# Order of the vector engine's operations in the stage that builds dense arrays of a graph network, and where loop bounds are loaded

## The chip, the cores and the metric

The kernel runs on one core of a Trainium2 chip. The metric is the device time of one execution in microseconds, lower is better. Five engines work side by side, each through its own program in order: PE (TensorE, matrix products into the PSUM banks), DVE (VectorE), ACT (ScalarE), POOL (GpSimd) and SP (SyncE, which issues DMAs). They meet at semaphores only.

## The reference

Four graph layers follow each other on a graph of 6250 nodes and 200,000 edges with 64 features a node. Each is added to its input and normalized over the features. Cut to what matters here:

```python
def prop(x):                                  # layer 0, Chebyshev, three times
    return segment_sum((x * norm)[src], dst, 6250) * norm
h = relu(concat(x[src], x[dst], edge_attr, u) @ W1 + b1)   # layer 1
agg = segment_sum(h, dst, 6250)
msg = edge_weight[:, None] * h[cols]          # layer 2, twice
h = segment_sum(msg, rows, num_segments=n)    # then a batch norm in Lorentz space
agg = segment_sum(h[src] * norm[:, None], dst, 6250)       # layer 3, graph convolution
```

The edges come sorted by dst, and dst is drawn as 6250 times a square of a uniform number, so nodes with a low number have many edges and the others few. The kernel turns the edge list into two dense arrays first: how often each source occurs for each destination (counts, for layers 0 and 3), and the sum of the edge weights for each pair (for layer 2). The sums over edges are then matrix products with these arrays.

## The kernel before, in words

The change lies in the stage that builds the two arrays (`build_dense` on DVE and PE, a loop on ACT, one on POOL). A **group** is five destinations; a source is split into a high part (50 values) and a low part (125), and a group has one PSUM bank. Two groups (`QUAD`) are a **block**, two blocks a **unit**: 1250 groups, 625 blocks, 313 units. The eight banks hold two units.

Edges stand 128 to a column. For the first column of every group everything is loaded ahead in `firsts`. A group with many edges needs more columns: these are the extra slots, **mores**, numbered `s` over the whole stage, each of which serves both groups of a block. How many a block has stands in the table `offs_sb`, which each engine reads into registers (`offs_of`, line 399, through `loads`, a TENSOR_LOAD whose line is 392). POOL picks the columns of a more out of the lists (`take`, line 655) into a ring of eight slots; it loads sixteen values of its own table for every five blocks (line 392 too).

The work of one unit, in the order of the engines' programs:

- DVE, `unit`: waits until `first_used` tells that PE is through with the unit two before, which used the same of two buffers (`first_planes`). Then `one_hots` (line 930, one operation of 1500 elements a partition) compares the keys with 0 to 124. Then `products` (line 937) multiplies the one-hots of the low part by three parts of the weight: one operation of 750 elements for each of the two blocks. Then the mores in order, each with `one_hots` (750 elements), a wait for it, and `products` (750). The one-hots of more `s` wait for `more_used`, that is until PE is through with more `s - 2`, and for POOL.
- PE, `unit`: loads the offsets once in two units, ahead of the first. `counts_of` (line 1653, one matmul of 250 columns a group, four a unit) needs the one-hots, and that ACT has copied the bank's last content out (`block_copied`). `weights_of` (line 1661, six matmuls a group, 24 a unit) needs the products; the last matmul of a block raises `first_used`. A more has two matmuls of line 1653 and twelve of line 1661, and the last raises `more_used`.
- ACT, `batch`: for each of five blocks waits until PE is through with it and its mores, and copies the weights (line 1424) and the counts (line 1425) out of the banks. It loads five offsets at the begin of a batch, and copies the degrees (line 1428) at its end. SP stores each batch of weights to DRAM, and counts after 25 blocks.

DVE loads its offsets once in two units too, ahead of the first one's one-hots. Semaphores raised ahead by POOL set the depths: `first_used` by 4 (two units), `more_used` by 2, `more_products` by 8, `block_copied` by 4.

## Time and profile before

| | |
|---|---|
| Median of 3 runs | 6696.05 us (6693.28 to 6703.47) |
| Profiled execution | 6737.52 us, span 6735.8 us |
| Mean granted TensorE clock | 0.761 |
| Busy over the span | PE 65%, PEld 50%, DVE 41%, POOL 30%, ACT 15% |
| The stage of the change | 190 us to 1995 us of the span |

How to read it. PE is the matmuls, PEld the weight loads beside them. The page cuts the span into 40 slices of 168 us; the stage of the change is slices 2 to 12. Busy counts an engine's operations, not its register work, branches, loads of registers (TENSOR_LOAD) or waits. In a timeline a row is one or several operations merged: start, time from the first's start to the last's end, engine, line, what is written and read, number, and in brackets the idle time before it with what ended it ("issue" is time in which the engine waited for nothing that the profile shows, such as its own register loads). T and X are the tiles in which the buffers lie: T those of units, X those of mores.

### The profile page before, as it was taken

What the parts mean: (1) busy time and instruction counts of PE and PEld (TensorE: products, weight loads), DVE (VectorE), ACT (ScalarE), POOL (GpSimd) and SP (SyncE); (2) the same over time, 40 slices, a digit from 0 to 9 for tenths busy, and PEclk for the clock granted to TensorE, in tenths of its full rate; (3) what the DMA queues carried; (4) which work ended last, traced back from release to release, by engine and by line L of the source; (5) the groups of instructions that cost most, each with busy time, mean ns of one, the idle gap of its engine ahead of it and who ended that gap; (6) DMA issues with size and microseconds to landing.
All of it is one profiled execution on the core that took longest, in us unless ns stands there. A gap on an engine that the chain in (4) does not pass through costs nothing.

```text
span 6735.8 us, 125070 instructions
## 1 busy us (share of the span) xinstructions
PE 4407.9 (65%) x39288; PEld 3374.0 (50%) x39289; DVE 2743.6 (41%) x4741; ACT 1043.5 (15%) x2060; POOL 2010.8 (30%) x2919
## 2 busy tenths in 40 slices
PE   1788888777669999625555555555555567657475
PEld 0566666666559899523333333333333343323275
DVE  8877777665551111323333333333333320020323
ACT  1012223355550000100000000000000000000100
POOL 2433332211000000055656656565656510000000
PEclk6899999988888999755555555555555569989887
DMA  2012333456766898352222222222222259969575
GB/s 74 9 56 71 105 105 112 127 176 218 221 215 267 345 377 348 121 98 61 61 60 61 61 61 61 61 61 61 61 60 61 61 199 418 371 284 418 230 291 194
DMA packets 443170, 1061.56 MB, mean 158 GB/s; under 512 B 127013, under 2 KB 285543, under 8 KB 414216
## 3 DMA queue, kind: packets, MB, share of 16 engines
q1 hardware_dynamic: 390985, 1003.20, 41.7%
q0 software_dynamic: 52096, 57.38, 4.2%
q8 instruction: 30, 0.49, 0.0%
q14 instruction: 59, 0.48, 0.0%
HBM read 815.58 MB, written 244.81 MB: 157 GB/s over the span
## 4 chain that ended last, share of the span: by engine, by line
PE 23%; issue 19%; DVE 19%; another core or an unknown queue 16%; DMA 9%; DVEq 6%; ACT 4%; ACTq 2%; SPq 1%; POOLq 1%; POOL 0%
PE banks L1627 12%; DMA T<-dense_w 8%; DVE X L930 4%; PE banks L1661 3%; DVE T L930 3%; PE banks L1712 2%; DVEq L392 2%; DVE WORK L1048 1%; ACTq L392 1%; DVE WORK L1032 1%; DVE WORK L1046 1%; PE banks L1653 1%; DVEq L930 1%; PE banks L1599 1%
## 5 line engine op out<-in xcount | busy, mean ns | idle before, releaser
L695 POOL DMA_INDIRECT WORK<-table,idx x1568 | 1523.2, 971 | 1880.2 <-DVE idx L1054 875.5
L1627 PE MATMUL banks<-WORK,T 125*128 125x192 bf16 (+1 forms) x10000 | 834.4, 247 | 61.8 <-DVE WORK L1098 61.8
L1627 PEld LDWEIGHTS banks<-WORK,T 125*128 125x128 bf16 (+1 forms) x10000 | 832.0, 99 | 64.2 <-issue 47.5
L1588 PE MATMUL banks<-W1c,WORK 128*128 128x128 f32 x1568 | 474.3, 429 | 463.3 <-issue 461.8
L1712 PE MATMUL banks<-T,WORK 125*64 125x391 f32 (+1 forms) x3200 | 575.3, 500 | 228.1 <-DMA T<-dense_w 186.2
L1584 PE MATMUL banks<-T,WORK 128*128 x1568 | 275.5, 293 | 639.3 <-issue 319.8
L1588 PEld LDWEIGHTS banks<-W1c,WORK 128*128 128x128 f32 x1568 | 382.5, 320 | 504.0 <-issue 503.8
L655 POOL TENSOR_TENSOR T<-T 128x6 f32 x1182 | 365.3, 331 | 837.1 <-DVE X L937 694.3
L1661 PE MATMUL banks<-X 128*128 128x125 bf16 x7092 | 549.2, 226 | 62.9 <-DVE X L937 57.6
L1661 PE MATMUL banks<-T 128*128 128x125 bf16 (+1 forms) x7500 | 576.6, 239 | 0.2 <-DVE T L937 0.2
L1661 PEld LDWEIGHTS banks<-T 128*128 128x128 bf16 x7500 | 538.6, 120 | 51.1 <-DVE T L937 42.4
L1661 PEld LDWEIGHTS banks<-X 128*128 128x128 bf16 x7092 | 460.2, 116 | 201.8 <-DVE X L937 192.2
L1584 PEld LDWEIGHTS banks<-T,WORK 128*128 128x128 bf16 x1568 | 219.3, 140 | 669.9 <-issue 664.2
L1424 ACT ACTIVATE WORK<-banks 125x504 f32<-125x504 f32 x625 | 378.1, 605 | 1106.0 <-PE banks L1661 981.4
L1712 PEld LDWEIGHTS banks<-T,WORK 125*64 125x64 f32 x3200 | 253.0, 137 | 549.4 <-issue 432.2
L1597 PE MATMUL banks<-WORK 128*128 128x128 bf16 x1568 | 429.3, 274 | 118.3 <-DVE WORK L1048 113.2
L1482 ACT ACTIVATE WORK<-WORK 128x512 bf16<-128x512 f32 x196 | 123.5, 630 | 2386.2 <-issue 1301.2
L1599 PE MATMUL banks<-WORK 128*64 128x128 bf16 x1568 | 464.6, 296 | 5.3 <-issue 5.3
L1032 DVE TENSOR_TENSOR WORK<-banks,WORK 128x512 f32<-128x512 f32 x196 | 135.6, 692 | 745.8 <-remote 624.1
L930 DVE TENSOR_TENSOR T<-X,NORM 128x1500 bf16<-128x1500 bf16 x313 | 294.5, 941 | 331.6 <-issue 183.4
L1653 PE MATMUL banks<-T 128*128 128x250 bf16 x1250 | 221.5, 298 | 313.7 <-DVE T L930 193.6
L1017 DVE TENSOR_TENSOR ACC<-ACC,banks 128x128 f32 x196 | 55.9, 285 | 808.6 <-remote 776.4
(369 smaller groups left out, 4777.7 us busy)
## 6 DMA issues: line engine op xcount, KB each, us to landing
T<-dense_c SPq DMA_DIRECT2D x200, 1562.5 KB, 8.4
T<-dense_w SPq DMA_DIRECT2D x200, 782.0 KB, 10.3
T<-dense_w SPq DMA_DIRECT2D x200, 780.5 KB, 10.4
dense_w<-WORK SPq DMA_DIRECT2D x125, 1093.8 KB
WORK<-rel_rows SPq DMA_DIRECT2D x197, 256.0 KB
WORK<-in_eaT SPq DMA_DIRECT2D x392, 128.0 KB
dense_c<-T SPq DMA_DIRECT2D x13, 3125.0 KB, 14.8
dense_c<-ACC SPq DMA_DIRECT2D x12, 3125.0 KB, 15.1
```

The costliest lines, as they stand in the source:

```text
L655: last = nc.gpsimd.tensor_tensor(quads[:, ds(slot, 1), :, t].rearrange("p s k -> p (s k)"), lists[:, :, ds(at[t], 1)].rearrange("p k c -> ...
L695: nc.gpsimd.indirect_dma_start(out=g_sb[:, u, c * D:(c + 1) * D], out_offset=None, in_=table, in_offset=bass.IndirectOffsetOnAxis(ap=idx[: ...
L930: return V.tensor_tensor(plane[:, 0:pairs * HOTS].rearrange("p (k n t) -> p k n t", n=LO, t=QUAD), iota2[:, 0:LO, :].unsqueeze(1).to_broad ...
L1424: C.activation(dense_out[0:LO, b0, 2 * b:2 * b + 2, :], both[:, :, KEYS:KEYS + 2 * WCOLS], ACT.Copy)
L1584: T.matmul(z, lhsT, QW12[:, ds(at * 2, P)], start=c in (0, 2), stop=False, skip_group_check=True)
L1588: last = T.matmul(z_sums[:, v, 2 * c * P:2 * (c + 1) * P].rearrange("p (c h f) -> p h c f", c=2, f=D)[:, 0, :, :], ea_sb[:, v, c * P:(c + ...
L1597: T.matmul(banks[:, v, 0:P], parts[:, v, c, 0:2 * D], hots[:, v, c // 2, :, c % 2], start=c == 0, stop=False, skip_group_check=True)
L1599: last = T.matmul(banks[0:D, v, 0:P], parts[:, v, c, 2 * D:3 * D], hots[:, v, c // 2, :, c % 2], start=False, stop=c == CHUNKS - 1, skip_g ...
L1627: last = T.matmul(banks[0:cols, 2 * u + s, 0:3 * D], a_rows[:, u, h * WAYS + s * LO:h * WAYS + s * LO + cols], x123[:, h, :], start=h == 0 ...
L1653: T.matmul(banks[:, bank, 0:KEYS], lows_view(plane, h)[:, t, :], hots_view(plane, h)[:, t, :], start=begins, stop=False, skip_group_check= ...
L1661: last = T.matmul(banks[:, bank, to - low:to + LO + high], keys_view(plane, h)[:, t, j, :], plane[:, first - QUAD * low:past + QUAD * high ...
L1712: last = [T.matmul(banks[c * D:(c + 1) * D, 4 * h + j, 0:n], lt[:, y, :], aw_sb[0:LO, 4 * y + 2 * h + c, j * PIECE:j * PIECE + n], start=f ...
```

## The change

On DVE the program is turned round. `products` takes all blocks of a unit in one operation of 1500 elements. The one-hots of unit 0 come ahead of the loop; in the loop come the one-hots of unit u+1, the products of unit u, in every second unit the load of offsets, and the mores of unit u. Of a pair of mores come both one-hots, then both products; a single more is done as before. `first_products` is raised once a unit, and PE waits for it once a unit. PE loads its offsets between the weights of the first of two units and their mores. ACT loads ten offsets for two batches at once in place of five for each.

```diff
--- before.py
+++ after.py
@@ -931,42 +931,59 @@
                                            iota2[:, 0:LO, :].unsqueeze(1).to_broadcast([P, 3 * pairs, LO, QUAD]),
                                            keys.unsqueeze(2).to_broadcast([P, 3 * pairs, LO, QUAD]), ALU.is_equal)
 
-                def products(plane, pairs, h, weights):
-                    first = products_of(pairs) + h * WEIGHTS
-                    low = plane[:, h * HOTS + QUAD * 2 * LO:(h + 1) * HOTS].rearrange("p (n t) -> p n t", t=QUAD)
-                    return V.tensor_tensor(plane[:, first:first + WEIGHTS].rearrange("p (k n t) -> p k n t", k=3, t=QUAD)[:, :, 0:LO, :],
-                                           low.unsqueeze(1).to_broadcast([P, 3, LO, QUAD]),
-                                           weights.unsqueeze(2).to_broadcast([P, 3, LO, QUAD]), ALU.mult)
-
-                def more(s, x):
-                    quad = quads[:, ds(s & (QRING - 1), 1), :, :].rearrange("p s k t -> p (s k) t")
+                def products(plane, pairs, weights):
+                    low = plane[:, 0:pairs * HOTS].rearrange("p (h k n t) -> p h k n t", k=3, n=LO, t=QUAD)[:, :, 2, :, :]
+                    return V.tensor_tensor(plane[:, products_of(pairs):planes_of(pairs)].rearrange("p (h k n t) -> p h k n t", k=3, n=WCOLS, t=QUAD)[:, :, :, 0:LO, :],
+                                           low.unsqueeze(2).to_broadcast([P, pairs, 3, LO, QUAD]),
+                                           weights.rearrange("p (h k) t -> p h k t", k=3).unsqueeze(3).to_broadcast([P, pairs, 3, LO, QUAD]), ALU.mult)
+
+                def quad_of(s):
+                    return quads[:, ds(s & (QRING - 1), 1), :, :].rearrange("p s k t -> p (s k) t")
+
+                def more_one_hots(s, x):
                     dve.wait_ge(quad_taken, s + 2)
                     dve.wait_ge(more_used, s + 1)
-                    one_hots(more_planes[:, x, :], 1, quad[:, 0:3, :]).then_inc(more_hots, 1)
+                    one_hots(more_planes[:, x, :], 1, quad_of(s)[:, 0:3, :]).then_inc(more_hots, 1)
+
+                def more_weights(s, x):
                     dve.wait_ge(more_hots, s + 1)
-                    products(more_planes[:, x, :], 1, 0, quad[:, 3:6, :]).then_inc(more_products, 1)
-
-                def unit(u, v, offs):
-                    plane, pairs = first_planes[:, v, :], UNIT // QUAD
+                    products(more_planes[:, x, :], 1, quad_of(s)[:, 3:6, :]).then_inc(more_products, 1)
+
+                pairs = UNIT // QUAD
+
+                def first_one_hots(u, v):
                     dve.wait_ge(first_used, u * pairs + pairs)
-                    one_hots(plane, pairs, firsts[:, 0, ds(u * pairs, pairs), :, :].rearrange("p b k t -> p (b k) t")).then_inc(first_hots, 1)
+                    one_hots(first_planes[:, v, :], pairs, firsts[:, 0, ds(u * pairs, pairs), :, :].rearrange("p b k t -> p (b k) t")).then_inc(first_hots, 1)
+
+                def first_weights(u, v):
                     dve.wait_ge(first_hots, u + 1)
-                    for h in range(pairs):
-                        products(plane, pairs, h, firsts[:, 1, ds(u * pairs + h, 1), :, :].rearrange("p b k t -> p (b k) t")).then_inc(first_products, 1)
+                    products(first_planes[:, v, :], pairs, firsts[:, 1, ds(u * pairs, pairs), :, :].rearrange("p b k t -> p (b k) t")).then_inc(first_products, 1)
+
+                def mores(offs):
                     dve.wait_ge(more_used, offs[0] + SLOTS)
                     dve.sem_inc(mores_begun, 1)
                     for h, (begin, past) in enumerate(zip(offs, offs[1:])):
                         with dve.If(past > begin):
                             with dve.Fori(begin, past, 2) as s:
-                                more(s, 2 * h)
                                 with dve.If(past > s + 1):
-                                    more(s + 1, 2 * h + 1)
-
+                                    for j in range(2):
+                                        more_one_hots(s + j, 2 * h + j)
+                                    for j in range(2):
+                                        more_weights(s + j, 2 * h + j)
+                                with dve.Else():
+                                    more_one_hots(s, 2 * h)
+                                    more_weights(s, 2 * h)
+
+                first_one_hots(dve.snap(0, min_val=0, max_val=0), 0)
                 with dve.Fori(0, UNITS // 2) as i:
-                    offs = offs_of(dve, i * 4, 5)
                     for v in range(2):
-                        unit(i * 2 + v, v, offs[2 * v:2 * v + 3])
-                unit(UNITS - 1, 0, offs_of(dve, BLOCKS - 1, 2))
+                        first_one_hots(i * 2 + (v + 1), 1 - v)
+                        first_weights(i * 2 + v, v)
+                        if v == 0:
+                            offs = offs_of(dve, i * 4, 5)
+                        mores(offs[2 * v:2 * v + 3])
+                first_weights(dve.snap(UNITS - 1, min_val=0, max_val=UNITS - 1), 0)
+                mores(offs_of(dve, BLOCKS - 1, 2))
                 end()
 
             def begin_rounds():
@@ -1409,9 +1426,8 @@
                 C.activation(to[:, 1, 0, :], got[:, 2, :], ACT.Copy).then_inc(firsts_copied, 1)
             end()
 
-            def batch(n, j, turn):
+            def batch(n, j, turn, past):
                 nth, slot, b0 = j // BATCHES // 2, j // BATCHES % 2, j % 2
-                past = offs_of(act, n * BATCH + 1, BATCH)
                 for b in range(BATCH):
                     d = (j % BATCHES * BATCH + b) * QUAD * GROUP
                     if b == 0:
@@ -1428,10 +1444,12 @@
                 C.activation(degp[0:LO, ds(n * SPAN, SPAN), :], dense_out[0:LO, b0, :, 0:2 * WCOLS:2 * WCOLS - 1], ACT.Copy).then_inc(degs_moved, 1)
 
             with act.Fori(0, STREAMS // 4) as i:
-                for j in range(4 * BATCHES):
-                    batch(i * (4 * BATCHES) + j, j, i)
+                for j in range(0, 4 * BATCHES, 2):
+                    past = offs_of(act, (i * (4 * BATCHES) + j) * BATCH + 1, 2 * BATCH)
+                    for k in range(2):
+                        batch(i * (4 * BATCHES) + (j + k), j + k, i, past[k * BATCH:])
             for j in range(BATCHES):
-                batch((STREAMS - 1) * BATCHES + j, j, STREAMS // 4)
+                batch((STREAMS - 1) * BATCHES + j, j, STREAMS // 4, offs_of(act, ((STREAMS - 1) * BATCHES + j) * BATCH + 1, BATCH))
             act.wait_ge(degs_moved, STREAMS * BATCHES)
             end()
             R = load(act, rounds_i[0:1, 0:1], 1, P)
@@ -1673,19 +1691,21 @@
                         last = weights_of(plane, 1, 0, t, bank + t)
                     last.then_inc(more_used, 1)
 
-                def unit(u, v, offs):
-                    plane, blocks = first_planes[:, v, :], len(offs) - 1
+                def unit(u, v, blocks):
+                    plane = first_planes[:, v, :]
                     pe.wait_ge(first_hots, u + 1)
                     for h in range(blocks):
                         pe.wait_ge(block_copied, u * 2 + (h + 1))
                         for t in range(QUAD):
                             counts_of(plane, h, t, UNIT * v + QUAD * h + t, True)
+                    pe.wait_ge(first_products, u + 1)
                     for h in range(blocks):
-                        pe.wait_ge(first_products, u * 2 + (h + 1))
                         for t in range(QUAD):
                             last = weights_of(plane, UNIT // QUAD, h, t, UNIT * v + QUAD * h + t)
                         last.then_inc(first_used, 1)
-                    with pe.If(offs[blocks] > offs[0]):
+
+                def mores(v, offs):
+                    with pe.If(offs[-1] > offs[0]):
                         for h, (begin, past) in enumerate(zip(offs, offs[1:])):
                             with pe.If(past > begin):
                                 with pe.Fori(begin, past, 2) as s:
@@ -1694,10 +1714,13 @@
                                         more(s + 1, 2 * h + 1, UNIT * v + QUAD * h)
 
                 with pe.Fori(0, UNITS // 2) as i:
-                    offs = offs_of(pe, i * 4, 5)
                     for v in range(2):
-                        unit(i * 2 + v, v, offs[2 * v:2 * v + 3])
-                unit(UNITS - 1, 0, offs_of(pe, BLOCKS - 1, 2))
+                        unit(i * 2 + v, v, 2)
+                        if v == 0:
+                            offs = offs_of(pe, i * 4, 5)
+                        mores(v, offs[2 * v:2 * v + 3])
+                unit(UNITS - 1, 0, 1)
+                mores(0, offs_of(pe, BLOCKS - 1, 2))
                 end()
 
             def dense_pass(l):
```

## Rows read from the trace of the kernel before

**Rows 1.** The page's part 1: busy us (share of the span) and instructions.

```profile
PE 4407.9 (65%) x39288; PEld 3374.0 (50%) x39289; DVE 2743.6 (41%) x4741; ACT 1043.5 (15%) x2060; POOL 2010.8 (30%) x2919
```

**Rows 2.** Windows: length; PE, PEld, DVE, ACT, POOL busy (count); PEclk; DMA; GB/s.

```profile
190.00:550.00 360.00, 305.90 (x3696) 235.02 (x3697) 279.13 (x518) 44.99 (x88) 143.05 (x468) 0.97 0.11 34
550.00:900.00 350.00, 304.39 (x3714) 240.00 (x3711) 271.39 (x486) 97.88 (x192) 118.75 (x370) 0.98 0.30 93
900.00:1455.00 555.00, 446.43 (x5306) 365.96 (x5306) 389.68 (x662) 210.04 (x421) 142.59 (x417) 0.93 0.41 131
1455.00:1995.00 540.00, 374.06 (x4315) 325.57 (x4312) 303.32 (x465) 321.06 (x676) 27.01 (x52) 0.88 0.68 213
```

**Rows 3.** The same windows, DVE line 930 alone: length, busy (count), PEclk, DMA.

```profile
190.00:550.00 360.00, 142.26 (x244) 0.97 0.11 34
550.00:900.00 350.00, 138.45 (x221) 0.98 0.30 93
900.00:1455.00 555.00, 193.36 (x283) 0.93 0.41 131
1455.00:1995.00 540.00, 145.79 (x156) 0.88 0.68 213
```

**Rows 4.** Timeline, two pairs of mores of the first unit.

```profile
224.76 0.93 PE L1661 MATMUL banks<-X 128*128 128x125 bf16 x12 [0.23 <-DVE X L937]
...
225.92 0.92 PE L1661 MATMUL banks<-X 128*128 128x125 bf16 x12
225.99 0.55 DVE L930 TENSOR_TENSOR X<-X,T 128x750 bf16<-128x750 bf16 x1
...
226.68 0.38 PE L1653 MATMUL banks<-X 128*128 128x250 bf16 x2
226.69 0.55 DVE L937 TENSOR_TENSOR X<-X,T 128x750 bf16<-128x750 bf16 x1
227.16 0.54 DVE L930 TENSOR_TENSOR X<-X,T 128x750 bf16<-128x750 bf16 x1
...
227.30 0.93 PE L1661 MATMUL banks<-X 128*128 128x125 bf16 x12 [0.24 <-DVE X L937]
...
228.53 0.55 DVE L930 TENSOR_TENSOR X<-X,T 128x750 bf16<-128x750 bf16 x1
```

**Rows 5.** Groups by line, last stretch: busy, mean ns | idle before, releasers.

```profile
L930 DVE TENSOR_TENSOR T<-X,NORM 128x1500 bf16<-128x1500 bf16 x153 | 144.1, 942 | 212.2 <-PE banks L1661 134.4 <-issue 77.3
...
L1653 PE MATMUL banks<-T 128*128 128x250 bf16 x610 | 115.4, 306 | 163.3 <-DVE T L930 75.8 <-ACT ACC L1425 40.4 <-ACT T L1425 35.5
...
L1653 PEld LDWEIGHTS banks<-T 128*128 128x128 bf16 x610 | 51.6, 108 | 197.1 <-ACT T L1425 78.1 <-ACT ACC L1425 63.1 <-issue 47.9
```

**Rows 6.** Line 392, register loads, last stretch: ns min/median/max, first and last start.

```profile
L392 DVEq TENSOR_LOAD <-X x76: 583/1974/3059, 1459.7 to 1988.5; - x76
L392 ACTq TENSOR_LOAD <-X x61: 540/2275/5810, 1457.0 to 1984.9; - x61
...
L392 POOLq TENSOR_LOAD <-X x52: 1057/2718/5303, 1454.9 to 1684.5; - x52
```

**Rows 7.** Timeline of ACT, its first copy after a load.

```profile
1755.43 0.59 ACT L1424 ACTIVATE WORK<-banks 125x504 f32<-125x504 f32 x1 [5.49 <-issue]
```

**Rows 8.** Timeline of units without mores.

```profile
1759.06 0.53 PE L1661 MATMUL banks<-T 128*128 128x126 bf16 x4
...
1759.73 0.94 DVE L930 TENSOR_TENSOR T<-X,NORM 128x1500 bf16<-128x1500 bf16 x1 [4.09 <-PE banks L1661]
...
1760.81 1.01 DVE L937 TENSOR_TENSOR T<-T,NORM 128x750 bf16<-128x750 bf16 x2
...
1761.96 0.63 PE L1653 MATMUL banks<-T 128*128 128x250 bf16 x4 [0.46 <-issue]
...
1762.43 1.63 PE L1661 MATMUL banks<-T 128*128 128x125 bf16 x24
```

**Rows 9.** Timeline of PE, weights of a unit at the lower clock.

```profile
1785.65 2.72 PE L1661 MATMUL banks<-T 128*128 128x125 bf16 x24
```

## The prediction, made before the change was built

> **What bounds the kernel now.** I read the page first: no engine is busy for more than 65% of the span [rows 1], so the answer lies in a stage. The change touches only the stage that builds the dense arrays, from 190 us to 1995 us, so I cut this stage into four stretches [rows 2]. Line 930 runs once for each unit and once for each extra slot, which I call a more [rows 3]. PE runs 28 matmuls for a unit and 14 for a more, so its count over 14 is twice the units plus the mores: 3696/14 = 264 in the first stretch, less 244, is 20 units and 224 mores. The others hold 44, 96 and 153 units with 177, 187 and 3 mores. A unit takes 18, 8.0, 5.8 and 3.5 us in the four.
>
> With mores, two engines hand to each other [rows 4]. PE ends a more's weights at 225.69 (224.76 + 0.93), DVE starts one-hots at 225.99, products 0.70 later, PE starts their weights 0.61 after that (227.30) and ends 0.93 later. That is 0.30 + 0.70 + 0.61 + 0.93 = 2.54 us, and the one-hots two mores apart start 2.54 apart (225.99, 228.53). So the wait on the more two back closes this loop; it is no engine's busy time.
>
> Without mores (the last stretch), three share the bound [rows 5]. DVE's idle before a unit's one-hots is 134.4 us for PE and 77.3 us "issue", which holds the load of five offsets (median 1.97 us there [rows 6]). PE's weight loads wait 78.1 + 63.1 = 141 us for ACT, and its matmuls 75.8 us for DVE. ACT stands for up to 5.49 us at a time where it loads [rows 7].
>
> **The change part by part.** (1) **The next unit's one-hots ahead of this unit's products.** DVE runs in program order. The one-hots of unit u+1 wait until PE is through the weights of unit u-1 (they share a buffer). Before, nothing but unit u+1 itself stood behind that wait; now the products of unit u stand behind it, and PE's weights of unit u wait for them. So a loop closes over one unit. The weights of u-1 end; 0.14 us later the one-hots of u+1 start (1759.06 + 0.53 to 1759.73 [rows 8]) and take 0.94. The products don't depend on them and start 0.08 before their end, as the one-hots at 227.16 do behind products of 0.55 that began at 226.69 [rows 4]; so 0.86. The products as one operation of 1500 elements get 0.94, that of the one-hots with as many elements; bounds 1.01 (the two now, overlapped) and 1.10 (twice 0.55). PE's weights of the first block used to follow the first 0.55 and now wait for all of it. Then 0.06 (0.61 less 0.55) and the weights 1.63 [rows 8]. Sum: 0.14 + 0.86 + 0.94 + 0.06 + 1.63 = **3.63 us a unit** as a floor, where 540/153 = 3.53 is the mean now, stalls included. PE's counts, 0.63, lie in the gap of 2.00 beside it.
>
> On top of the floor: the clock. At the lower clock the weights take 2.72 [rows 9]; the granted clock of the stretch is 0.88 [rows 2], so 24% of it is at 1.2 GHz, 0.24 x 1.09 = 0.26; I take 0.2, since some of it falls in idle time. PE's load and ACT, below, get 0.1 and 0.2. So 4.13 us a unit, 153 x 4.13 = 632 us against 540: **+92 us**. Lower bound 3.63 throughout, +15; upper bound with ACT's whole wait kept, 141/153 = 0.92 instead of 0.2, 4.85 us, +202.
>
> (2) **Mores in pairs: one-hots, one-hots, products, products.** The second one-hots of a pair need the more just before the pair to be used, and the first products now stand behind them. The loop over a pair becomes: release 0.30, one-hots to products 0.47 (independent), products to weights 0.61, weights to the next counts 0.76 (225.92 to 226.68), two counts 0.24 (half of the 0.47 that four take, 1761.96 to 1762.43 [rows 8]), weights 0.92: **3.30 us for two mores** instead of 2.54 [rows 4]. In exchange DVE's own time for a pair falls by 0.46 (four starts 0.47 apart instead of 0.70 and 0.47 in turn), which helps only where PE is not waited for. POOL, which waits for products to reuse a slot, gets the first of a pair 0.47 later; it may be eight slots ahead, so I add nothing (without that cover 0.24 a more). A unit of two pairs, from the end of its own weights: DVE had time for the first pair while PE did the weights, so PE does it at its rate, 0.24 + 0.92 + 0.76 + 0.24 = 2.16; the second ends 3.30 later, 5.46; the next unit's counts start 0.16 before that and its weights end 0.47 + 1.63 later, 7.40. PE now loads its offsets between weights and mores, where the mores wait for it. Where it loads today it stands for 0.46 [rows 8]; more branches follow here, so I double that, an estimate: 0.9 in two units, 0.45 a unit, 7.9 in all. First stretch: 20 x 7.9 + (224 - 80)/2 x 3.30 = 158 + 238 = 396 against 360, **+36 us**. Second: 44 x 7.9 + 0.5 x 3.30 = 350, **0**. By the same steps a unit with three mores takes 6.6, one with two 4.6, one with one or none about 4.0. The third stretch runs from three down to none, 1.9 on average, mixed: 5.2 against 5.8, 96 x 5.2 = 499 against 555, **-56**. Bounds of these three together: +36 if few mores gain nothing, -75 if the first stretch loses nothing and the gain is a third larger.
>
> (3) **DVE's load behind products.** DVE loads once in two units, 0.58 to 3.06 us [rows 6], and idles. Behind the queued one-hots and products (0.86 + 0.94) it is hidden but for the longest. The trace has no DVE load beside a running operation, so the cover could be missing; then it costs what it costs now. In the last stretch this gives nothing in any case: DVE waits there for PE in the loop of (1), with 1.8 us a unit to spare. The gain of the third stretch contains it.
>
> (4) **ACT loads ten offsets once in ten blocks, not five in five.** Sixteen values cost POOL 1.06 us and five cost 0.54 to 0.58 [rows 6], so undisturbed two loads become one for 0.3 us less in five units. But ACT's median is 2.28 and its longest 5.81 while the stores run; if ten values cost twice five, nothing is saved and the stall comes in one piece. The counts of a unit may start 1.4 us late in the loop of (1) (2.00 less 0.63) before it shows. I take 0.2 a unit, between 0 and 0.92. The Trainium skill ("Runtime: NRT & Kernel Launch", Instruction fetch mechanics) gives about 200 ns a register for such loads; five more values would be 1.0 us more, where the rows give 0.04 us a value ((1.06 - 0.58)/11). By that rule ACT's stall comes in one piece, which is rival C; the rows of undisturbed loads speak against it, ACT's own median of four times its shortest for it.
>
> Sum: 92 + 36 + 0 - 56 = **+72 us**. The profiled execution took 6737.52 (span 6735.8), so it would be 6810; the median of the runs is 6696.05, 0.6% below, and the same difference gives **6768 us**.
>
> **The rivals.** A, the forecast, 57%: own range +30 to +130. B, **faster**: PE is so far ahead that the wait on unit u-1 doesn't bite, and DVE's hidden load and ACT's fewer loads show. A unit would be bound by PE's 0.63 + 1.63 or ACT's 2.10 of work (321/153 [rows 2]) with its loads, about 3.0: 153 x 3.0 = 459, -81, with -56 and +36 together -101: 6595. For it: DVE's idle of 77.3 us on issue. Against: it decides only if PE's weights of u-1 end more than 1.8 us before PE could start those of u, and the order on DVE leaves no way to that. A weaker form, the floor with no stall (+15) and the mores at their lower bound (-75), gives 6636. Together 13%. C, **ACT takes over**: loads of ten cost twice, 5 to 11 us, more than two units of banks can cover; the last stretch goes to 4.85 us a unit, +202 in place of 92: 6878. 15%. D, **the lower clock**: PE idles 1.4 us in each unit; if the clock stayed at 1.2 GHz, weights of 2.72 make a unit 3.63 + 1.09 = 4.72, +182 in place of 92: 6858. 5%. E: gains and costs cancel within 0.2%, 10%.
>
> **How the numbers follow.** A measurement can tell about 0.2%, 13 us, from no change. Faster 0.13 (B), same 0.10 (E), slower 0.77 (A, C, D). The range leaves out most of B and the top of C: 6680 to 6880.
>
> **What would show it.** In the last stretch DVE's one-hots should follow PE's last weights by 0.14 with products right behind, PE's weights should start 0.06 behind products, and starts of one-hots should stand 3.6 to 4.2 apart; DVE's idle on "issue" should be gone and PE's idle on DVE grow from 75.8 to over 150 us. In the first unit, pairs should repeat every 3.30 us. ACT should load 65 times in the stage instead of 125; loads over 5 us each point to C. It is wrong if the last stretch is under 3.5 us a unit, or pairs stay at 2.5.

## The result and the profile after

The changed kernel takes **6889.8 us** (median of 4 runs, 6887.6 to 6892.4); before measured beside it 6696.7. The ratio is 1.0287, 95% interval 1.0269 to 1.0305: slower by 193 us, where +72 was forecast, and 10 us above the end of the range. The profiled execution spans 6886.9 us. The page's part 1 of after, to hold against [rows 1]:

```profile
PE 4362.3 (63%) x39288; PEld 3375.5 (49%) x39289; DVE 2658.6 (39%) x4428; ACT 1047.1 (15%) x2060; POOL 2042.4 (30%) x2919
```

PE and ACT have the work of before, DVE has 313 operations and 85 us less; what has grown is waiting. Windows of after, the same four stretches moved to where their units now run (columns as in [rows 2]):

```profile
190.00:585.00 395.00, 289.44 (x3608) 236.32 (x3609) 259.42 (x488) 42.50 (x83) 129.24 (x459) 0.98 0.10 31
585.00:945.00 360.00, 289.41 (x3731) 246.33 (x3730) 255.32 (x446) 96.78 (x192) 128.85 (x377) 0.98 0.28 87
945.00:1505.00 560.00, 436.94 (x5324) 363.06 (x5321) 368.63 (x571) 209.71 (x422) 169.67 (x422) 0.95 0.42 131
1505.00:2175.00 670.00, 405.20 (x4302) 335.98 (x4302) 275.60 (x310) 322.62 (x666) 24.08 (x51) 0.81 0.54 170
```

The matmuls of the four (16,965, in [rows 2] 17,031) count out to nearly the same work; the first stretch ends a few us before its twentieth unit does. In the rows of after, lines 936, 1671, 1679, 1440 and 1441 are what lines 937, 1653, 1661, 1424 and 1425 are in before. The last stretch has grown by 130 us and its granted clock has fallen from 0.88 to 0.81.

For an exact comparison I take as marks the start of the first products of units 0, 20, 64, 160 and 312 in each trace; "slot" below is the time from one mark to the next. Before: **353, 354, 554, 535**, sum 1796. After: **397, 360, 562, 668**, sum 1987, so +44, +6, +8, +133: 191 of the 193 us lie in the stage. Differences of a few us between two kernels in one slot say nothing by themselves: each is one profiled execution.

**The loop over one unit is there as forecast.** Timeline of after, last stretch, at a place where ACT isn't loading (ACT, POOL and PEld rows left out):

```profile
1887.01 0.62 PE L1671 MATMUL banks<-T 128*128 128x250 bf16 x4
...
1887.31 0.94 DVE L930 TENSOR_TENSOR T<-X,NORM 128x1500 bf16<-128x1500 bf16 x1 [1.86 <-PE banks L1679]
...
1888.17 0.93 DVE L936 TENSOR_TENSOR T<-T,NORM 128x1500 bf16<-128x1500 bf16 x1
...
1889.16 1.65 PE L1679 MATMUL banks<-T 128*128 128x125 bf16 x24 [1.54 <-DVE T L936]
...
1890.97 0.94 DVE L930 TENSOR_TENSOR T<-X,NORM 128x1500 bf16<-128x1500 bf16 x1 [1.86 <-PE banks L1679]
```

From one-hots to products 0.86, to PE's weights 0.99, these 1.65, and 0.16 later the next one-hots: 3.66 us a unit. The forecast's floor was 3.63. In 67 of the 152 units of the last slot the one-hots follow each other at 3.66 to within 0.02, and in none at less than 3.64. Before, they followed at 2.27 in the commonest case, the second unit of two, for which DVE has nothing to load.

**ACT's stall and the clock lie on top of it.** A load of ten offsets runs here between two rows of ACT:

```profile
1759.49 2.22 PE L1679 MATMUL banks<-T 128*128 128x125 bf16 x24 [0.68 <-DVE T L936]
1761.51 1.03 PE L1671 MATMUL banks<-T 128*128 128x250 bf16 x4
...
1763.70 2.71 PE L1679 MATMUL banks<-T 128*128 128x125 bf16 x24 [1.16 <-DVE T L936]
...
1769.04 0.59 ACT L1440 ACTIVATE WORK<-banks 125x504 f32<-125x504 f32 x1 [10.27 <-issue]
...
1770.16 0.60 PE L1671 MATMUL banks<-T 128*128 128x250 bf16 x2 [3.75 <-ACT ACC L1441]
...
1771.52 2.61 PE L1679 MATMUL banks<-T 128*128 128x125 bf16 x24
...
1774.28 0.94 DVE L930 TENSOR_TENSOR T<-X,NORM 128x1500 bf16<-128x1500 bf16 x1 [5.92 <-PE banks L1679]
```

ACT stands for 10.27 us, longer than the two units whose banks are free last, and PE idles 3.75 us for it. And PE, with gaps in front of its counts and of its weights, does a unit's weights in 2.71 us (1.2 GHz) in place of 1.65 (2.4 GHz). The loads of after in this stretch, columns as in [rows 6]:

```profile
L392 DVEq TENSOR_LOAD <-X x76: 580/1358/2966, 1512.4 to 2174.9; - x76
...
L392 ACTq TENSOR_LOAD <-X x32: 559/5381/10277, 1514.0 to 2166.3; - x32
```

32 loads in place of 61 (in the whole stage 65 in place of 125, as said), but the median has gone from 2.28 to 5.38 us.

**Idle time of the last stretch.** Waits of DVE, 1510 to 2160 us (us in total, times, longest):

```profile
DVE T L930 <- PE banks L1679: 384.1, 147, 9.7
```

Groups of PE's matmuls and of DVE's one-hots, 1505 to 2175 us, columns as in [rows 5]:

```profile
L1679 PE MATMUL banks<-T 128*128 128x125 bf16 x2416 | 289.5, 250 | 126.1 <-DVE T L936 125.6
...
L930 DVE TENSOR_TENSOR T<-X,NORM 128x1500 bf16<-128x1500 bf16 x152 | 143.5, 944 | 393.1 <-PE banks L1679 393.1
...
L1671 PE MATMUL banks<-T 128*128 128x250 bf16 x608 | 121.7, 324 | 137.3 <-ACT T L1441 56.2 <-ACT ACC L1441 52.7 <-DVE T L930 21.7
```

DVE's 77.3 us on "issue" of [rows 5] are gone, but nothing is won by that: DVE waits 393 us for PE here (134.4 before), while PE waits 125.6 + 21.7 = 147 us for DVE (before 75.8), just short of the 150 that I named. Each waits for the other in turn: that is the closed loop.

**The pairs** of the first unit, timeline (POOL and PEld left out), against [rows 4]:

```profile
225.91 0.89 PE L1679 MATMUL banks<-X 128*128 128x125 bf16 x12
...
227.11 0.55 DVE L930 TENSOR_TENSOR X<-X,T 128x750 bf16<-128x750 bf16 x1 [0.41 <-POOL T L655]
227.58 1.00 DVE L936 TENSOR_TENSOR X<-X,T 128x750 bf16<-128x750 bf16 x2
...
228.18 0.92 PE L1679 MATMUL banks<-X 128*128 128x125 bf16 x12 [1.02 <-DVE X L936]
...
229.16 0.89 PE L1679 MATMUL banks<-X 128*128 128x125 bf16 x12
...
230.36 0.55 DVE L930 TENSOR_TENSOR X<-X,T 128x750 bf16<-128x750 bf16 x1 [0.41 <-POOL T L655]
```

Release 226.80 to 227.11, products 0.47 later, weights 0.60 later, and so on: 230.36 - 227.11 = 3.25 us a pair, forecast 3.30. The row names POOL as what ended the wait, but the wait for `more_used` passes 0.04 us behind the end of PE's weights both times, so it was PE.

### The profile page after: what moved, and what is told of

Its sections match the earlier page's. It is cut to its first block, busy times and chain, and to the rows that moved or that the text cites. A ratio compares the mean times of both kernels' runs of the same rounds, so it can differ in the third digit from the quotient of the medians.

```text
span 6886.9 us, 124604 instructions
## 1 busy us (share of the span) xinstructions
PE 4362.3 (63%) x39288; PEld 3375.5 (49%) x39289; DVE 2658.6 (39%) x4428; ACT 1047.1 (15%) x2060; POOL 2042.4 (30%) x2919
## 4 chain that ended last, share of the span: by engine, by line
PE 28%; DVE 19%; another core or an unknown queue 18%; issue 12%; DMA 9%; DVEq 5%; ACTq 3%; ACT 2%; POOLq 2%; SPq 1%; POOL 1%
PE banks L1645 12%; DMA T<-dense_w 8%; PE banks L1679 7%; ACTq L392 2%; PE banks L1735 2%; DVEq L392 2%; DVE WORK L1065 2%; DVE T L936 2%; DVE X L936 2%; DVE WORK L1049 1%; PE banks L1617 1%; DVE X L930 1%; PE banks L1615 1%; DVE WORK L1052 1%
## 5 line engine op out<-in xcount | busy, mean ns | idle before, releaser
L655 POOL TENSOR_TENSOR T<-T 128x6 f32 x1182 | 395.8, 357 | 862.8 <-DVE X L936 606.1
L1679 PEld LDWEIGHTS banks<-X 128*128 128x128 bf16 x7092 | 487.8, 116 | 255.6 <-DVE X L936 247.4
L1615 PEld LDWEIGHTS banks<-WORK 128*128 128x128 bf16 x1568 | 163.5, 104 | 911.3 <-issue 768.4
L1606 PE MATMUL banks<-W1c,WORK 128*128 128x128 f32 x1568 | 434.0, 432 | 141.7 <-issue 140.6
L930 DVE TENSOR_TENSOR X<-X,T 128x750 bf16<-128x750 bf16 x591 | 319.3, 552 | 359.5 <-PE banks L1679 169.1
L1606 PEld LDWEIGHTS banks<-W1c,WORK 128*128 128x128 f32 x1568 | 366.4, 325 | 134.4 <-issue 133.8
```

Source lines behind the costliest of these rows:

```text
L655: last = nc.gpsimd.tensor_tensor(quads[:, ds(slot, 1), :, t].rearrange("p s k -> p (s k)"), lists[:, :, ds(at[t], 1)].rearrange("p k c -> ...
L930: return V.tensor_tensor(plane[:, 0:pairs * HOTS].rearrange("p (k n t) -> p k n t", n=LO, t=QUAD), iota2[:, 0:LO, :].unsqueeze(1).to_broad ...
L1606: last = T.matmul(z_sums[:, v, 2 * c * P:2 * (c + 1) * P].rearrange("p (c h f) -> p h c f", c=2, f=D)[:, 0, :, :], ea_sb[:, v, c * P:(c + ...
L1615: T.matmul(banks[:, v, 0:P], parts[:, v, c, 0:2 * D], hots[:, v, c // 2, :, c % 2], start=c == 0, stop=False, skip_group_check=True)
L1679: last = T.matmul(banks[:, bank, to - low:to + LO + high], keys_view(plane, h)[:, t, j, :], plane[:, first - QUAD * low:past + QUAD * high ...
```

## The experiments

Each ratio is to the kernel before on the same chip. The slots are 0 to 20, 20 to 64, 64 to 160, 160 to 312, in us. Code that only follows from an edit (definitions split, line moves) is left out of the diffs. Extra values that ACT loads are not used. The first four kernels ran on a chip on which the kernel before takes 6157.9 us in all, the others on chips on which it takes 6731 to 6740. The stage takes the same on all: where a kernel leaves a slot's work alone, the slot comes out within 6 us of before's (ACT ten alone 353, 354, 558; pairs alone 536 in the last). Outside the slots up to 13 us more separate a kernel from before (branches alone, 104 by the ratio and 91 in the slots); no run explains these.

| kernel | ratio (95%) | slots | sum against 1796 |
|---|---|---|---|
| order alone | 1.0056 (1.0040 to 1.0073) | 348, 339, 536, 600 | +27 |
| pairs alone | 1.0157 (1.0140 to 1.0174) | 410, 367, 572, 536 | +89 |
| one operation alone | 1.0033 (1.0022 to 1.0045) | 362, 358, 560, 534 | +18 |
| ACT ten alone | 1.0126 (1.0109 to 1.0143) | 353, 354, 558, 600 | +69 |
| branches alone | 1.0156 (1.0138 to 1.0173) | 389, 381, 580, 537 | +91 |
| DVE's load alone | 0.9972 (0.9960 to 0.9984) | 352, 352, 555, 522 | -15 |
| after, ACT five | 1.0197 (1.0180 to 1.0214) | 399, 356, 553, 612 | +124 |
| after, PE's load first | 1.0281 (1.0264 to 1.0298) | 399, 348, 557, 679 | +187 |
| after, mores as before | 1.0178 (1.0160 to 1.0195) | 346, 344, 543, 668 | +105 |
| order and DVE's load | 1.0011 (1.0000 to 1.0021) | 344, 334, 527, 596 | +5 |
| ACT from a multiple of four | 0.9982 (0.9973 to 0.9992) | 354, 352, 552, 518 | -20 |
| ACT eight | 0.9954 (0.9939 to 0.9969) | 354, 354, 552, 505 | -31 |
| ACT eight, DVE's load | 0.9948 (0.9934 to 0.9961) | 350, 352, 554, 505 | -35 |
| the same, PE's load | 0.9935 (0.9920 to 0.9950) | 351, 353, 550, 502 | -40 |
| split order | **0.9880** (0.9863 to 0.9896) | 346, 334, 523, 501 | -92 |

### One part of the change at a time, on the kernel before

**The order alone.**

```diff
+first_one_hots(0, 0)
 with dve.Fori(0, UNITS // 2) as i:
     offs = offs_of(dve, i * 4, 5)
     for v in range(2):
+        first_one_hots(i * 2 + (v + 1), 1 - v)
         unit(i * 2 + v, v, offs[2 * v:2 * v + 3])
```

`unit` here has products and mores only.

> The kernel before with one edit: the one-hots of unit u+1 come ahead of the products of unit u. Products stay two operations, mores, DVE's, PE's and ACT's loads stay as before. I count the stage in units 0 to 19, 20 to 63, 64 to 159 and 160 to 311; before they take 353, 354, 554 and 535 us, in the changed kernel 397, 360, 562 and 668. Theory (the loop over one unit): the last stretch gets a floor of 0.14 + 0.86 + 0.55 + 0.06 + 1.63 = 3.24 us a unit (PE's weights start behind the first of the two products) and with clock and ACT about 3.8, so 580 us, +45; the first three move by less than 10 each; in all +30 to +60, about 6740. Rival (ACT's loads of ten cause the loss, the order is harmless or hides something): the last stretch stays within 10 of 535 or falls.

Measured: -5, -15, -18, +65. Units with mores gain from the order, units of the last slot lose 0.43 us each. The floor is there: 49 of 151 distances between one-hots in the last slot lie at 3.25 to 3.32, forecast 3.24. What lies on top of it was put too low, 3.8 a unit where 3.95 was measured; the granted clock of the slot is 0.82, before 0.88.

**Pairs alone.** The `mores` of the diff above, with `Else`, on the old order.

```diff
-more(s, 2 * h)
 with dve.If(past > s + 1):
-    more(s + 1, 2 * h + 1)
+    for j in range(2):
+        more_one_hots(s + j, 2 * h + j)
+    for j in range(2):
+        more_weights(s + j, 2 * h + j)
+with dve.Else():
+    more_one_hots(s, 2 * h)
+    more_weights(s, 2 * h)
```

> The kernel before with one edit: of a pair of mores both one-hots come first, then both products; a single more has its own branch. Theory (the two mores' loop closes one more earlier): pairs of the first unit repeat every 3.3 us instead of 2.54, +40 us in the first stretch, +10 in the second. For the third stretch, where the forecast failed, two theories: if the extra branch and register work of the single more costs DVE's time (0.5 us a single), it takes +20 to +40; if the trouble there is the order over units or PE's load, it stays within 10. Last stretch 535 unchanged.

Measured: +57, +13, +18, +1, a pair every 3.25 us in most cases.

**The products of a unit in one operation.**

```diff
-for h in range(pairs):
-    products(plane, pairs, h, ...).then_inc(first_products, 1)
+products(plane, pairs, ...).then_inc(first_products, 1)
```

> The kernel before with one edit: the products of a unit in one operation of 1500 elements, one semaphore step a unit, PE waits for it once. Theory: an operation of 0.94 us in place of two that take 1.01 together, so DVE gains 0.07 a unit, and PE's first weights start 0.39 later; where DVE or ACT sets the pace neither shows: within 15 us of before in all. Rival (the merged operation alone costs 0.39 a unit wherever PE waits for DVE): +20 to +60, most of it in the last two stretches.

Measured: +9, +4, +6, -1, ratio 1.0033: a small loss of 18 us, just above the 15 expected, in the slots with mores. PE begins a unit's weights later, and DVE saves 0.07 us.

**ACT loads ten.**

```diff
-for j in range(4 * BATCHES):
-    batch(i * (4 * BATCHES) + j, j, i)
+for j in range(0, 4 * BATCHES, 2):
+    past = offs_of(act, (i * (4 * BATCHES) + j) * BATCH + 1, 2 * BATCH)
+    for k in range(2):
+        batch(i * (4 * BATCHES) + (j + k), j + k, i, past[k * BATCH:])
```

> The kernel before with one edit: ACT loads ten offsets for two batches instead of five for each. In the changed kernel these loads took 2.6, 5.4 and 10.1 us (shortest, median, longest in the last stretch), against 0.54, 2.28 and 5.81. Theory (a load costs by the value and its stall comes in one piece): the last stretch grows by 20 to 60 us, the first two not at all, ACT's loads as in the changed kernel. Rival (half as many loads help, since ACT has fewer stops): the last stretch falls by 10 to 40.

Measured: 0, 0, +4, **+65**. Its loads and its clock (0.82, before 0.88):

```profile
L392 ACTq TENSOR_LOAD <-X x33: 560/5369/10012, 1460.2 to 2053.7; - x33
```

```profile
1455.00:2055.00 600.00, 388.64 (x4299) 337.93 (x4297) 300.88 (x462) 321.43 (x668) 25.94 (x52) 0.82 0.61 191
```

So this part costs much the same without the new order. The four parts add up to +61, +2, +10, +130 against the whole change's +44, +6, +8, +133, which also moves DVE's and PE's loads. In the first slot they don't add: 17 us are missing.

**The branches alone.** Mores in the old order, but with the branches of the pairs.

```diff
-more(s, 2 * h)
 with dve.If(past > s + 1):
+    more(s, 2 * h)
     more(s + 1, 2 * h + 1)
+with dve.Else():
+    more(s, 2 * h)
```

> The kernel before with the branch form of the changed one, the order of operations kept: if a pair is left, one-hots, products, one-hots, products, else the single more. The pairs edit alone gave 410, 367, 572 and 536 us against 353, 354, 554 and 535. Theory A (order makes the pairs slow, branches make the singles slow): first stretch within 5 of 353 with pairs at 2.54, third stretch +10 to +20. Theory B (all comes from the order): all within 5.

Measured: **+36, +27, +26, +2**, as much as the pairs together, with the same operations in the same order. Its timeline (PE, PEld, POOL left out):

```profile
226.59 0.54 DVE L930 TENSOR_TENSOR X<-X,T 128x750 bf16<-128x750 bf16 x1
...
227.29 0.55 DVE L937 TENSOR_TENSOR X<-X,T 128x750 bf16<-128x750 bf16 x1
...
228.28 0.55 DVE L930 TENSOR_TENSOR X<-X,T 128x750 bf16<-128x750 bf16 x1 [0.44 <-POOL T L655]
...
228.98 0.55 DVE L937 TENSOR_TENSOR X<-X,T 128x750 bf16<-128x750 bf16 x1
```

Products to the next pair's one-hots take 0.99 us, before 0.68: the jump over the `Else`, the loop's jump and the test now lie between them, where before the test stood beside a running operation. A pair takes 2.85 in place of 2.54. Put on top of this, pairing itself gives +21, -14, -8. The gain is not where I forecast it, in units with few mores: in the third slot a unit with three takes 7.47 here and 7.23 with pairs alone, one with two 6.05 and 6.09, one with one 4.84 and 4.89. Of the 28 units with two mores, 27 have one for each block, so they hold no pair at all. Beside the gain the branches cost more than all of it.

### Parts undone in the changed kernel

**After, with ACT's loads of five.** The inverse of the fourth diff.

> The changed kernel with ACT's loads as before, five offsets for each batch. The four stretches (units 0 to 19, 20 to 63, 64 to 159, 160 to 311) take 397, 360, 562 and 668 us in the changed kernel. Theory (the parts add up: ACT's ten alone gave +65 in the last stretch, the order alone +65): the last stretch falls by 55 to 70, to about 605, the others by less than 5. Rival (behind the loop over one unit ACT has room, so its loads cost nothing there; the forecast's 0.2 us a unit): it falls by less than 30.

Measured: last slot 668 to 612, clock of the stretch 0.81 to 0.87. Ten against five offsets is 56 us here, 65 on before.

**After, with PE's load ahead of the unit's counts.**

```diff
 with pe.Fori(0, UNITS // 2) as i:
+    offs = offs_of(pe, i * 4, 5)
     for v in range(2):
         unit(i * 2 + v, v, 2)
-        if v == 0:
-            offs = offs_of(pe, i * 4, 5)
         mores(v, offs[2 * v:2 * v + 3])
```

> The changed kernel with PE's load of offsets back at the begin of two units, ahead of their counts, instead of between weights and mores. Theory (in the third stretch the mores wait for that load on PE, and DVE's entry to the next mores waits for PE to be through with them): the third stretch falls from 562 by 15 to 40, the second from 360 by 10 to 20, the last by less than 10. Rival (the third stretch's loss is DVE's branches and the pairs): under 10 in each.

Measured, against after: +2, -12, -5, +11. Where it stands makes no difference in the sum; the ratio's interval overlaps that of after. The sum hides two effects in the third slot: with the load first, a unit with one more takes 4.76 in place of 5.13, and one with none 4.38 in place of 3.98.

**After, with the mores as before**: one after the other, old branches.

> The changed kernel with one part undone: the mores are done one after the other with the branches of before, everything else as changed. Theory (the pair and its branches cost the first two stretches, and their sum with order, loads and one operation is additive): stretches of the changed kernel 397, 360, 562, 668 go to 345-360, 338-355, 525-545 and 660-670, ratio to before 1.016 to 1.022, nearly all of what is left in the last stretch. Rival (in the third stretch the wait of DVE for all earlier mores, with PE's load ahead of them, is what took the expected gain): third stretch stays at 550 or more.

Measured: 346, 344, 543, 668, so pairs with their branches are 51 + 16 + 19 + 0 = **86 us** of the 191, and the first three slots without them are 28 us under before. The last is untouched: what is left, +133, is all there.

### What the third slot and the last were worth

**DVE's load alone**, behind the first unit's products in the old order.

```diff
-offs = offs_of(dve, i * 4, 5)
 for v in range(2):
-    unit(i * 2 + v, v, offs[2 * v:2 * v + 3])
+    unit(i * 2 + v, v)
+    if v == 0:
+        offs = offs_of(dve, i * 4, 5)
+    mores(offs[2 * v:2 * v + 3])
```

`unit` here has one-hots and products only.

> The kernel before with one step of the change alone: DVE loads its offsets behind the products of the first of two units, ahead of its mores, and the order of one-hots and products stays as it was. Theory 1 (a load behind queued work is hidden, and the wait of one-hots on PE stays free of it): the 77 us of DVE idle on issue in the last stretch go, and with PE and ACT sharing the bound about a third of it shows: last stretch 535 to 505-525 us, third 554 to 530-545, first and second within 5. Ratio 0.993 to 0.998. Theory 2 (the load only moves: where mores follow, they wait for it instead, and without mores ACT's loads are late next): last stretch 530-537, third 550-560, ratio 0.998 to 1.001.

Measured: 352, 352, 555, 522. The last slot is as theory 1 had it, the third as theory 2. There gains and losses cancel: units without mores take 2.90 (before 3.35) and with three 6.88 (7.09), but with one 4.93 (4.68) and with two 5.91 (5.80), since their mores now stand behind the load.

**The order and DVE's load.** Both diffs together.

> The kernel before with the next unit's one-hots ahead of this unit's products, and DVE's load of offsets behind those products. The order alone gave 348, 339, 536, 600. Theory 1 (with the order changed the load is hidden behind queued work, which is the gain forecast for the third stretch): third 515 to 528, second 330-337, last 590-602; DVE's idle on issue ahead of one-hots of units under 10 us. Theory 2 (the load then stands ahead of the unit's mores, and these wait for it; the loop over the pair of mores and PE sets the pace): third 532-545, second 335-345.

Measured: 344, 334, 527, 596. DVE's group of a unit's one-hots in 900 to 1400 us:

```profile
L930 DVE TENSOR_TENSOR T<-X,NORM 128x1500 bf16<-128x1500 bf16 x93 | 87.9, 946 | 45.2 <-PE banks L1672 34.4 <-issue 9.9
```

Idle on issue is 9.9 us there; before it was 62.2 for 83 units. The load is hidden there, and against the order alone that is worth 9 us in the third slot (536 to 527) and 5 in the second. Half of it comes back ahead of the unit's mores: they had 22.9 us on issue before (20.1 with the order alone) and have 46.9 here.

### Cheaper loads, and a kernel faster than both

**ACT loads from a multiple of four on**, five to eight values.

```diff
-past = offs_of(act, n * BATCH + 1, BATCH)
+skip = (j * BATCH + 1) % 4
+past = offs_of(act, n * BATCH + (1 - skip), BATCH + skip)[skip:]
```

> The kernel before with ACT's load of a batch starting at the last multiple of four values (5 to 8 values instead of 5; the extra ones are not used). In the kernel before, every fourth of these loads takes 0.54 us, the one that starts at such a multiple, and the others 2.2 to 2.3, while DVE's and PE's, which always start there, take 0.58. Theory (a load that doesn't start at a multiple of four values is fetched value by value): undisturbed loads of ACT fall to 0.55 to 0.65 us, all of them, and those under full DMA traffic from 5.2 to about 2.1; the last stretch, 535 us in the kernel before, falls by 20 to 60. Rival (the 2.2 us come from the batch's DMA, which starts with the load): loads stay at 2.2 and the time too.

Measured: last slot 535 to 518, just short of the 20 to 60 us expected. The loads follow each other with 6, 7, 8 and 5 values, and their medians over units 20 to 159 are 0.76, 1.6, 0.56 and 0.55 us. More values can be cheaper.

**ACT loads eight aligned values always** (in the diff, `8` for `BATCH + skip`).

> The kernel before, but ACT always loads eight values that begin at a multiple of four, and uses the five it needs. Theory (what an ACT load costs is the number of its reads, four aligned values each, and each read is slow once the batch's DMA runs): all of its loads in the last stretch take 0.55 to 0.6 us, where five values from a multiple of four on took 0.55, eight 0.56, seven 1.6 and misaligned five 2.3. Last stretch 518 (aligned start, five to eight values) to 505-515 us, others within 4 of before, ratio 0.995 to 0.998. Rival (time follows the number of values, or the stores next to it): loads stay at 0.56 to 1.6 mixed, last stretch 515-535.

Measured: last slot 505, at the lower end of what the theory gave, clock 0.90.

```profile
L392 ACTq TENSOR_LOAD <-X x61: 541/552/3222, 1455.2 to 1953.6; - x61
```

The median is 0.55 us, in place of 2.28; a few still reach 3.2.

**Both loads**, ACT's eight and DVE's behind the products.

> The kernel before with DVE's load behind the first unit's products and ACT's eight aligned values, nothing else of the change. If the two loads are separate causes of the last stretch's idle time, the gains add: last stretch 535 to 480-500 us, third 554 to 530-545, ratio 0.988 to 0.993. If PE's own work with its load and the block copies is late next, they don't add: last stretch 500-515, ratio 0.993 to 0.996.

Measured: last slot 505 again. The gains don't add: both loads filled the same idle time.

**The same, and PE's load between weights and mores.**

> As the kernel with both loads mended, and PE's load of offsets between the weights of the first of two units and their mores, as the change has it. Theory (there the mores wait for PE's load, 0.3 to 0.5 us once in two units, and DVE's wait for all earlier mores stands behind it too): first, second and third stretch 5 to 12 us longer than with the two loads alone, last 0 to 8 shorter, ratio 0.001 to 0.004 above that kernel's. Rival (the load is hidden behind PE's queued weights): first three stretches within 3, last 5 to 15 shorter, ratio at or below that kernel's.

Measured: 351, 353, 550, 502, ratio 0.9935 beside 0.9948, the intervals overlap. The theory's 5 to 12 us more in each of the first three slots aren't there, as the rival said. The last slot is 3 us shorter, where the rival said 5 to 15; so small a difference can't be told from none.

**The order split by mores.**

```diff
+first_one_hots(dve.snap(0, min_val=0, max_val=0), 0)
+with dve.Fori(0, 160 // 2) as i:
+    for v in range(2):
+        first_one_hots(i * 2 + (v + 1), 1 - v)
+        first_weights(i * 2 + v, v)
+        if v == 0:
+            offs = offs_of(dve, i * 4, 5)
+        mores(offs[2 * v:2 * v + 3])
+with dve.Fori(160 // 2, UNITS // 2) as i:
+    for v in range(2):
+        first_weights(i * 2 + v, v)
+        if v == 0:
+            offs = offs_of(dve, i * 4, 5)
+        mores(offs[2 * v:2 * v + 3])
+        first_one_hots(i * 2 + (v + 1), 1 - v)
```

In the second loop the one-hots come last, which is the order of before. ACT loads eight aligned values, everything else is as before.

> The order of the change where there are mores and that of before where there are none: for units 0 to 159 the next unit's one-hots come ahead of this unit's products, from unit 160 on behind them; DVE's load behind the products, ACT loads eight aligned values. Theory (the order gains by what a unit with mores has waiting, and costs only through the loop over one unit where there are none): stretches 346-350, 335-341, 520-538, 503-508, the stage 60 to 90 us under before's 1796; ratio 0.987 to 0.992. Rival (the gains of order and loads overlap, both fill the same idle time): stage 1745-1760, ratio 0.992 to 0.995.

Measured: **6646.7 us, ratio 0.9880**, slots 346, 334, 523, 501. Windows of its last two slots:

```profile
873.00:1395.00 522.00, 423.23 (x5282) 364.41 (x5280) 379.10 (x660) 211.26 (x420) 164.39 (x418) 0.94 0.44 139
1395.00:1895.00 500.00, 358.56 (x4287) 314.19 (x4285) 299.77 (x462) 320.42 (x666) 25.60 (x53) 0.90 0.73 228
```

The order's gain (first three) and its loss (last) are separable by whether a unit has mores, and the gains of order and loads add: -9, -20, -27 of order and DVE's load in the first three and -30 of ACT's eight in the last make -86, measured -92. By the two ratios it is 4.0% faster than the changed kernel (0.9880/1.0287 = 0.9604).

## Why the prediction was right in sign and too low in size

By its own steps, in units' time per slot: forecast 396, 350, 499, 632, sum 1877; measured 397, 360, 562, 668, sum 1987. Of the 191 us, 72 were forecast, 110 lie between these two sums, and 9 are the difference between the forecast's base (the windows of [rows 2], 1805) and the slots of before, 1796. The 110 have these places: 1, 10, 63 and 36 us in the four slots. The step that failed most is the one on units with few mores in the third stretch. The mechanism of the last stretch was right, and the terms on top of its floor, ACT's stall above all, were too small.

- **The first stretch and the pair's loop, right.** 396 against 397, 3.30 against 3.25 us. The pair and its branches there cost 51 us (397 to 346), more than the +36, since the rest of the change gives back 7 (353 to 346). The second stretch, forecast 350, came to 360. On the old order the branches account for 36 of the pairs' 57. In the loop over a pair no branch shows: it takes the 3.25 us that the operations alone give, since DVE waits for PE twice in it and the jumps fall into these waits.
- **The third stretch, wrong by 63 us: the largest miss.** The step was "a unit with three mores takes 6.6, one with two 4.6, one with one or none about 4.0". The means of the third slot, in us a unit (five more units have four):

| mores | units | forecast | before | order and DVE's load | after, mores as before | after |
|---|---|---|---|---|---|---|
| 0 | 12 | 4.0 | 3.35 | 3.74 | 3.95 | 3.98 |
| 1 | 21 | 4.0 | 4.68 | 4.47 | 4.97 | 5.13 |
| 2 | 28 | 4.6 | 5.80 | 5.30 | 5.25 | 5.63 |
| 3 | 30 | 6.6 | 7.09 | 6.56 | 6.78 | 6.89 |

  One and two mores are 1.1 and 1.0 us too low, 53 of the 63 us. The sum took the first two mores for a pair that DVE has ready while PE does the unit's weights. But 27 of the 28 units with two mores have no pair, and PE does wait for DVE at the mores. Groups of PE in after, 945 to 1505 us:

```profile
L1679 PE MATMUL banks<-X 128*128 128x125 bf16 x1506 | 168.6, 231 | 34.5 <-DVE X L936 33.0
...
L1671 PE MATMUL banks<-X 128*128 128x250 bf16 x376 | 78.3, 291 | 37.6 <-DVE X L930 21.0 <-issue 16.3
```

  Three costs stood at nothing or too low. The pairs with their branches take 0.2 and 0.4 of the 1.1 and 1.0 (after against mores as before). PE's moved load takes 0.4 of a unit with one more, which units with none give back. And the wait that opens the mores, shown in a timeline of after:

```profile
1408.79 1.66 PE L1679 MATMUL banks<-T 128*128 128x125 bf16 x24 [0.29 <-DVE T L936]
...
1412.15 0.60 PE L1671 MATMUL banks<-X 128*128 128x250 bf16 x2 [1.71 <-issue]
...
1412.55 1.46 PE L1679 MATMUL banks<-X 128*128 128x125 bf16 x12
...
1414.64 1.99 PE L1679 MATMUL banks<-T 128*128 128x125 bf16 x24
...
1415.36 0.55 DVE L930 TENSOR_TENSOR X<-X,T 128x750 bf16<-128x750 bf16 x1 [2.98 <-issue]
```

  PE's load stands for 1.71 us ahead of the more; its weights end at 1414.01, and only then DVE passes the wait that opens `mores` (for all mores before this unit), and needs another 1.35 us of register work and jumps to the next more's one-hots at 1415.36. I had that wait in the code and left it out of the sum. It is in every kernel here and no run leaves it out, so its share isn't shown. But order and DVE's load, without pairs, branches, PE's moved load or ACT's ten, still stand 0.5 and 0.7 above the forecast for one and two mores, so nearly half of the one miss and two thirds of the other lie neither in the branches nor in PE's load. The gain that I named, the hidden load, is real but small: 9 us, and 27 with the order.
- **The last stretch, 36 us too low, with the mechanism right.** The floor was 3.63 and is 3.66. On top of it I put 0.2 for the clock, 0.1 for PE's load, 0.2 for ACT; 668/152 is 4.39 us, so it is 0.74 in place of 0.5. The clock: I kept the 0.88 of before, and it fell to 0.81; the order alone took it to 0.82. PE's weights of a unit take 1.99 us in the mean of this slot (before 1.88), 0.34 above 1.65, so the clock's term is 0.34 in place of 0.2. PE's load: nothing measurable (with PE's load first the slot was 11 us longer, not shorter). ACT and what remains: 0.40. I treated the clock and ACT as separate terms. They aren't: with loads of five in place of ten the slot loses 56 us and its clock rises from 0.81 to 0.87.
- **ACT's ten offsets: the mis-sized term.** I took 0.3 us saved in five units where undisturbed, and a stall "in one piece" if ten cost twice five. They do: median 5.38 against 2.28. The price is 56 us in after and 65 alone, where all of ACT stood at 0.2 us a unit, 31. The 0.54 to 0.58 of [rows 6] were not the undisturbed load but the one that starts at a multiple of four, every fourth of ACT's; from the other starts the medians over units 20 to 159 are 2.28 to 2.32 us. Rival C was right on the load (over 5 us each) and put its price too high, +202 for the stretch in place of the measured +133; I read this as two units of free banks holding much of each stall. That its total, 6878, lies nearest to the 6889.8 measured is luck: its last stretch is 74 us too long, and the first three are 74 too short in all. Its rows, [rows 7] and [rows 6], a median four times the shortest, spoke for it from the start. The Trainium skill ("Runtime: NRT & Kernel Launch", Instruction fetch mechanics) gives about 200 ns a register. These traces don't agree: by that figure, as an estimate, eight values would take 1.6 us and ten 2.0, where eight took 0.557 and ten 5.38 in the median.
- **What DVE's load behind products does, right**: it runs beside the queued operations (in after a load from 1417.18 to 1419.10 us beside products from 1417.72 to 1418.66), and without mores it gives nothing in the new order (600 to 596).
- **Rivals B, D, E** fell: DVE waited for PE 147 times between 1510 and 2160 us, 384 us in all, so the wait on unit u-1 bit in nearly every unit; the clock fell in part only; gains didn't cancel costs.

Open: why in after the second slot moves by 12 us with PE's load, and how the +44, +6, +8 split exactly between branches and pairing, as the branches alone were tried on the old order only; and how much of a unit with few mores is the wait that opens them.

## What to carry to other kernels

Ask of an operation pulled ahead of another what it waits for, and who waits for the one now behind it: in one program order the wait closes a loop, and its length (here 3.66 us) can be summed from rows of before. Pulling work ahead paid in units that have something else queued (-38 us in the first three slots) and cost in units that don't (+65), so split the loop where the kind of unit changes. Before giving a kind of unit a price, count how many of them have what the price rests on (here a pair). Count jumps and register loads of a hot loop like operations, and price a stall of an engine that frees buffers together with the clock that the waiting TensorE loses.

## What the runs showed that I had not expected

- **The time of a register load depends on where it starts, and more values can be cheaper.** Five values cost ACT 0.55 us from a multiple of four on and 2.28 to 2.32 (medians) from the other three places; eight from such a multiple 0.557, six 0.76, seven 1.6, and ten from other places 5.38 in the median. A reading, not tried by itself: a load that starts at a multiple of four takes its values in fours, one read each, and single values besides; any other load takes all of them one by one. It gives the order of ACT's times, but not that seven cost ACT 1.6 and sixteen cost POOL 1.06, which would both be four reads if POOL's starts at a multiple of four. Why the same load takes up to 5.8 us in places isn't settled.
- **An `Else` costs on the path.** 0.31 us a pair of mores, +91 us in the stage with no operation changed: as much as the edit to pairs, which has the same branches.
- **The granted clock depends on more than TensorE's own work**, which is the same in all kernels. In the last slot it is 0.88 before, 0.82 with the order alone and 0.82 with ACT's ten alone, 0.81 in after and 0.87 there with ACT's five, 0.90 in the kernels whose ACT loads take 0.55 us (0.92 in one of them). It doesn't follow the slot's length alone: 0.82 at 600 us and 0.87 at 612, 0.81 and 0.79 at 668. Which of the waits lowers it isn't settled.
